# Two reorderings in a two-layer transformer kernel: value heads among the projections, and row scores behind a projection

## What is computed

```python
x = layernorm(x + attn0(x))   # 32 heads of width 16; the scores of a token are head against head
x = layernorm(x + ffn0(x))    # three dense layers with sign matrices, relu between
x = layernorm(x + attn1(x))   # 32 heads, rotary, causal, window of 128 tokens
x = layernorm(x + ffn1(x))    # 16 experts, top 2, and a shared expert

# attn0
q, k, v = (x @ w.T + b for each).reshape(1, 1024, 32, 16)
scores = einsum("bshd,bstd->bsht", q, k) / 4
context = einsum("bsht,bstd->bshd", softmax(scores), v)
```

## Time and profile before

| | us |
|---|---|
| runs before: median of 3 | 741.8 (741.8 to 742.43) |
| the profiled execution, its time | 742.59 |
| its span | 740.7 |
| PE busy | 618.5 (84%) |
| VectorE busy | 388.8 (52%) |
| ScalarE busy | 277.7 (37%) |
| GpSimd busy | 236.5 (32%) |
| mean granted clock of PE | 0.907 |

### The profile page before, as it was taken

How to read it: one execution, slowest core, us unless ns; L and a number is a source line. 1 busy time by engine, 2 the same in 40 slices (tenths; PEclk the granted TensorE clock), 3 DMA queues, 4 the chain that set the end, 5 groups by cost and what they waited for, 6 DMA issues and landing times.

```text
span 740.7 us, 13453 instructions
## 1 busy us (share of the span) xinstructions
PE 618.5 (84%) x5108; PEld 487.0 (66%) x5108; DVE 388.8 (52%) x1120; ACT 277.7 (37%) x439; POOL 236.5 (32%) x347
## 2 busy tenths in 40 slices
PE   2998996648889886989898987778689899999984
PEld 2997985536677664766676665556448688878761
DVE  4324345285776766758585766561546043322354
ACT  5156046356644143334342533344620022221313
POOL 6003422354200235445352634354005511111062
PEclk9999999688999986989898999576889999999997
DMA  8921213323016727263452719120005859997455
GB/s 292 401 94 34 50 31 100 79 56 94 1 60 153 141 74 145 79 95 114 61 144 31 171 40 213 22 67 23 1 1 177 334 198 395 418 417 291 184 169 185
DMA packets 49360, 104.37 MB, mean 141 GB/s; under 512 B 12113, under 2 KB 18385, under 8 KB 47761
## 3 DMA queue, kind: packets, MB, share of 16 engines
q1 hardware_dynamic: 30032, 61.68, 23.4%
q0 software_dynamic: 13744, 31.61, 18.8%
q10 hardware_dynamic: 5520, 10.23, 3.8%
HBM read 63.77 MB, written 35.13 MB: 134 GB/s over the span
## 4 chain that ended last, share of the span: by engine, by line
PE 56%; DVE 11%; DMA 11%; ACT 9%; issue 7%; POOL 6%; SPq 1%; POOLq 0%; ACTq 0%; DVEq 0%
PE bank L331 14%; PE bank L508 10%; PE bank L367 10%; ACT FP L1427 3%; DVE FP L902 3%; PE bank L594 3%; PE bank L579 3%; DMA slots_out<-FP 3%; PE bank L566 3%; PE bank L378 2%; POOL slots_in L1825 2%; POOL FP L1837 2%; DMA QS<-QS 2%; PE bank L389 2%; PE bank L709 2%
## 5 line engine op out<-in xcount | busy, mean ns | idle before, releaser
L1427 ACT ACTIVATE FP<-bank 128x512 f32<-128x512 f32 (+1 forms) x250 | 145.8, 624 | 324.2 <-PE bank L579 132.5
L1160 DVE CUSTOM_DVE_ANT_0 kraw<-bank,maskb 128x256 bf16<-128x256 f32 (+1 forms) x256 | 88.5, 401 | 60.6 <-PE bank L566 60.6
L508 PE MATMUL bank<-W,XR 128*128 128x512 f32 x348 | 106.0, 450 | 0.1
L331 PE MATMUL bank<-FP 128*128 128x128 f32 x558 | 87.5, 311 | 1.3 <-ACT FP L1427 1.3
L367 PE MATMUL bank<-W,XR 128*128 128x512 f32 x288 | 78.9, 420 | 6.1 <-DVE W L902 5.2
L508 PEld LDWEIGHTS bank<-W,XR 128*128 128x128 f32 x348 | 71.1, 216 | 16.3 <-DVE XR L902 0.5
L1789 POOL TENSOR_SCALAR_AFFINE_SELECT FP<-FP 128x512 f32<-128x512 f32 x64 | 41.4, 669 | 114.3 <-ACT FP L1427 114.3
L367 PEld LDWEIGHTS bank<-W,XR 128*128 128x128 f32 x288 | 63.7, 271 | 11.8 <-DVE W L902 5.6
L331 PEld LDWEIGHTS bank<-FP 128*128 128x128 f32 x558 | 65.2, 192 | 3.5 <-issue 1.8
L902 DVE TENSOR_TENSOR FP<-FP,bank 128x128 f32<-128x128 f32 (+1 forms) x39 | 14.4, 369 | 70.5 <-ACT FP L1427 45.7
L331 PE MATMUL bank<-RP,W 128*128 128x512 f32 x192 | 47.5, 404 | 4.4 <-DVE FP L902 2.2
(11 more groups left out here) (164 smaller groups left out, 1021.9 us busy)
## 6 DMA issues: line engine op xcount, KB each, us to landing
FP<-in_experts_dram SPq DMA_DIRECT2D x31, 768.0 KB, 7.1
slots_out<-QS SPq DMA_DIRECT2D x48, 256.0 KB, 2.7
FP<-slots_in POOLq DMA_DIRECT2D x31, 256.0 KB, 6.5
slots_out<-FP ACTq DMA_DIRECT2D x31, 256.0 KB, 7.7
slots_in<-RP SPq DMA_DIRECT2D x7, 1024.0 KB, 13.3
RP<-slots_out POOLq DMA_DIRECT2D x16, 384.0 KB, 5.7
QS<-slots_out POOLq DMA_DIRECT2D x10, 384.0 KB, 8.4
FP<-in_shared_dram SPq DMA_DIRECT2D x4, 768.0 KB, 7.5
```

The costliest lines, as they stand in the source:

```text
L331: mm = nc.tensor.matmul(bank, lhs, rhs, start=(n == 0), stop=(n == len(terms) - 1))
L508: mm = nc.tensor.matmul(b[:, :], *terms[n], start=(n == 0), stop=(n == len(terms) - 1))
L1160: ins = nc.vector.tensor_tensor_reduce(masked[:, 2 * (f % 2) + m, 0:n], b[:, m, :], maskb[:, m0:m0 + n], 1.0, -BIG, ALU.add, ALU.max, hmax ...
L1427: return nc.scalar.activation(o, i, func, **kw)
```

## The change

*First attention, TensorE.* Heads of keys of group 0 go three to a projection; the heads of values of group 0 go to the S banks, and the first two scores stand among the x transposes. Group 1's projections lie two to a step up to step 2 and one to a step in steps 3 to 6 (`tiles_of`); the heads of queries and keys stand two behind each third of a projection; the heads of values all stand in step 7, in V and A banks. VectorE drains the value heads of group 0 and two of the four of group 1 (`values_out`). *Key diagonals.* Five buffers: steps 0 to 9 use two as before, steps 10 to 15 three others (the third is zeroed by GpSimd after the last biased row), so SyncE waits for `scores(k - 3)` there. *ScalarE.* `ak` and `aq` are loaded in eight pieces of 256 KB behind step 9, 10, 11 and 12, not in step 4; `conn_weights(0)` moves ahead of the first statistics, `conn_weights(1)` goes one quarter to a step; the rounded pieces move to steps 13 and 14, beside `hidden(0, 1)`, and behind `hidden_out(1, 0, 0)`. GpSimd forms its eight remainders after step 15. *Second attention.* In iterations 0 to 5 `row_scores(r, 0)` stands behind the first projection; in iteration 6 (`late`) every row-score group comes one step later, with what follows from its maxima.

```diff
-        kdiag = [[t[:, a + 2048 * n:a + 2048 * n + 2048] for n in range(2)] for t, a in ((WF, 6 * DC * D), (FP, 0))]
+        kdiag = [t[:, a:a + 2048] for t, a in ((WF, 6 * DC * D), (WF, 7 * DC * D), (FP, 0), (FP, 2048), (RPF, 3264))]
...
+        def key_slot(k):
+            return (k % 2, k // 2 + 1) if k < NCH + 2 else (2 + (k - NCH - 2) % 3, (k - NCH - 2) // 3 + 1)
+        tiles_of = [tiles_between[a:b] for a, b in ((2, 4), (4, 6), (6, 8), (8, 9), (9, 10), (10, 11), (11, 12))]
# TensorE, first attention
             for j in range(G):
                 project(0, 2, j)
-                to_heads(V, 0, 1, 2 * j, 2 * j + 1)
+                to_heads(V, 0, 1, *range(3 * j, min(3 * j + 3, H // 4)))
...
-                to_heads(A, 0, 2, j, j + 1)
-            for k in range(2):
-                scores(k)
-                project(*tiles_between[k])
+                to_heads(S, 0, 2, j, j + 1)
+                scores(j // 2)
+            project(*tiles_between[0])
+            project(*tiles_between[1])
             for k in range(2 * NCH):
                 if k + 2 < 2 * NCH:
                     scores(k + 2)
-                between(k, 0)
-                if k in (6, 7):
-                    to_heads(V, 1, 2, 2 * k - 12, 2 * k - 11)
+                if k < 3:
+                    project(*tiles_of[k][0])
+                elif k < 5:
+                    for part in range(2):
+                        project(*tiles_of[k][0], 3 * part, 3)
+                        to_heads(V, 1, k - 3, 2 * part, 2 * part + 1)
+                elif k < 7:
+                    project(*tiles_of[k][0])
+                elif k == 7:
+                    for a in range(0, HD // 4, 2):
+                        to_heads(V, 1, 2, a)
+                        to_heads(A, 1, 2, a + 1)
...
                 values(k)
-                between(k, 1)
+                if k < 3:
+                    project(*tiles_of[k][1])
+                elif k < 5:
+                    for part in range(2, 4):
+                        project(*tiles_of[k][0], 3 * part, 3)
+                        to_heads(V, 1, k - 3, 2 * part, 2 * part + 1)
# TensorE, second attention (VectorE's row_maxima in the same way)
+                t, r, d, late = i + 2, i + 1, i - 1, int(i == T - 2)
                 for s in range(8):
-                    if r < T:
-                        row_scores(r, s)
+                    if r < T and (s > 0 or i < 0) and s >= late:
+                        row_scores(r, s - late)
...
                     if s < 2 and 2 <= t < T:
                         project2(t, 1 - s)
+                    if s == 0 and 0 <= i < T - 2:
+                        row_scores(r, 0)
...
+                if i == T - 2:
+                    row_scores(r, 7)
# SyncE
-                if k >= 2:
+                if 2 <= k < NCH + 2:
                     C.filled(sp, ("scores", k - 2))
+                elif k >= NCH + 5:
+                    C.filled(sp, ("scores", k - 3))
...
+                if k == NCH + 4:
+                    sp.wait_ge(diag_zero, 4)
...
-                if k == NCH + 5:
+                if k == NCH + 4:
                     load_kernel(1, k1)
# VectorE
+            def values_out(ring, g, a):
+                b = ring.take(v, ("heads", g, 2, a))
+                nc.vector.tensor_copy(vT[:, :, 4 * a:4 * a + 4].rearrange("p s h -> p h s"),
+                                      b[:, :].rearrange("p (h s) -> p h s", h=4)).then_inc(ring.free, 1)
# ScalarE
+            def load_piece(m):
+                n, c = (0, 2)[m // 4], m % 4
+                nc.scalar.dma_start(raw_c[n][:, c * D:(c + 1) * D], (ak, aq)[m // 4][c * P:(c + 1) * P, :]).then_inc(wc_in[n], 16)
...
             exponentials(NCH + 1)
-            high_piece(0)
-            high_piece(1)
+            C.filled(s, ("scores", NCH + 1))
+            conn_weights(0)
+            A.drained(s, ("heads", 1, 2, HD // 4 - 1))
+            load_piece(0)
+            load_piece(1)
             roots(slice(0, G), 0)
             exponentials(NCH + 2)
+            load_piece(2)
+            load_piece(3)
             s.wait_ge(offset_ready, 1)
             for t in range(G):
                 normalise(t)
-            conn_weights(0)
             for k in range(11, 2 * NCH):
                 exponentials(k)
+                if k <= 12:
+                    load_piece(2 * k - 18)
+                    load_piece(2 * k - 17)
...
-                if k <= 13:
-                    high_piece(2 * k - 20)
-                    high_piece(2 * k - 19)
-                if k == 14:
-                    conn_weights(1)
+                if k <= 14:
+                    conn_weights(1, k - 11)
+                if k in (13, 14):
+                    high_piece(2 * k - 26)
+                    high_piece(2 * k - 25)
...
-            hidden_out(0, 1, *range(DC))
-            high_piece(8)
-            high_piece(9)
+            for o in range(DC):
+                hidden_out(0, 1, o)
+                high_piece(4 + o)
...
-            high_piece(10)
-            high_piece(11)
+            for m in range(8, 12):
+                high_piece(m)
# GpSimd
+                if k == 7:
+                    A.drained(p, ("rows", 1, 2, G - 1))
+                    nc.gpsimd.memset(RPF[:, 3264:5312], 0.0).then_inc(diag_zero, 1)
+            for m in range(8):
+                low_piece(m)
```

More of the change, by code:

```diff
@@ L267, in build @@
         diag_zero = sem("diag_zero")
-        kdiag_in = [sem(f"kdiag_in{n}") for n in range(2)]
+        kdiag_in = [sem(f"kdiag_in{n}") for n in range(5)]
         kq_split = sem("kq_split")
@@ L383, in scores @@
                 g, c = chunk(k)
[L384 removed]
+                slot, n = key_slot(k)
+                pe.wait_ge(kdiag_in[slot], 16 * G * n)
                 b = C.fill(pe, ("scores", k))
[L386 removed]
+                keys = kdiag[slot].rearrange("p (j g a h) -> p j g a h", j=G, g=4, a=4)
                 for a in range(4):
@@ L656, in _ @@
                         A.drained(pe, ("ffn", T - 1))
-                    if s == 5 and r < T:
+                    if s == 5 + late and r < T:
                         turn_maxima(r, 0)
@@ L1055, in _ @@
                 low_xt(("x", G + j), every_fourth(j))
-            A.drained(v, ("heads", 0, 2, HD // 4 - 1))
-            shift(0)
+                if j == 1:
+                    for a in range(HD // 4):
+                        values_out(S, 0, a)
+                    shift(0)
             rows_biased(*tiles_between[0])
@@ L1224, in _ @@
             for i in range(-1, T):
-                t, r, d = i + 2, i + 1, i - 1
+                t, r, d, late = i + 2, i + 1, i - 1, int(i == T - 2)
                 for s in range(8):
-                    if r < T:
-                        row_maxima(r, s)
+                    if r < T and (s > 0 or i < 0) and s >= late:
+                        row_maxima(r, s - late)
                     if s < 2 and d >= 0:
                         context_divided(U, d, s)
+                    if s == 0 and 0 <= i < T - 2:
+                        row_maxima(r, 0)
                     if s == 1 and 2 <= t < T:
@@ L1239, in _ @@
                         rope_sum(t, 0)
-                    if s == 3 and r < T:
+                    if s == 3 + late and r < T:
                         maxima_split(r, 0)
@@ L1255, in _ @@
                         low_dense(("x2", t + 1), xa[t + 1][1], xa[t + 1][0])
-                    if s == 7 and r < T:
+                    if s == 7 and r < T and late == 0:
                         maxima_split(r, 1)
@@ L1484, in _ @@
             heads_out(V, 0, 1, *range(H // 4))
-            A.drained(s, ("rows", 0, 2, G - 1))
-            for j in range(0, G, 2):
+            for j in range(G):
                 high_x(G + j)
-                high_x(G + j + 1)
-                heads_out(A, 0, 2, j, j + 1)
             exponentials(0)
@@ L1728, in _ @@
             nc.gpsimd.memset(RPF[:, 0:3 * 1088], 0.0).then_inc(diag_zero, 1)
-            A.drained(p, ("heads", 0, 2, HD // 4 - 1))
+            S.drained(p, ("heads", 0, 2, HD // 4 - 1))
             p.wait_ge(pool, 3)
@@ L1744, in _ @@
                 if k == NCH:
-                    V.drained(p, ("heads", 1, 2, HD // 4 - 1))
+                    V.drained(p, ("heads", 1, 2, HD // 4 - 2))
+                    A.drained(p, ("heads", 1, 2, HD // 4 - 1))
                 for g in range(4):
@@ L1802, in _ @@
             for i in range(-1, T):
-                t, r = i + 2, i + 1
+                t, r, late = i + 2, i + 1, int(i == T - 2)
                 for step in range(8):
@@ L1817, in _ @@
                         stack_rows(t, 0)
-                    if step == 6 and r < T:
+                    if step == 6 + late and r < T:
                         stack_maxima(r, 0)
```

55 lines of the change are left out of this document (21 added, 34 removed).

## The result

The changed kernel is slower: 752.69 us, median of four runs (749.95 to 755.98), against 741.88 (741.8 to 742.43) for the kernel before. The ratio is 1.0146, 95% interval 1.0099 to 1.0193. The forecast was 744.8 in a range of 737 to 751: right in sign, too small in size, and the time is outside the range.

What follows compares the result with a forecast made beforehand. TensorE was 56% of the chain, losing time to first-attention diagonal waits. First half −11.1, second attention +11.8, clock +1.9, late form +0.4: +3.0 us on 742.59 gives 745.6, 744.8 as median; range 737 to 751.

Steps and rivals of the forecast that it cites:

- First attention: Whole first half: −6.7 up to values of step 8, −5.0 to step 15, +0.6 after; −11.1 us, range −6 to −14.
- The wait left: TensorE's 6.74 us wait for the key diagonal of step 8 was to shrink to 1.5 us.
- the third head's wait: Three key heads per projection, two V banks: the third head waits some 0.9 us, twice, costing 1.9 us.
- the wait for the value diagonal of step 8: First attention, TensorE: this wait, 4.29 us before, was to stay at some 4 us.
- The third buffer: Third key-diagonal buffer: removes the 3.42 us wait at step 14 and its issue behind the kernel load.
- Order of the transfers: Second attention boundaries: maxima stay behind the stack, so key scores start as now or slightly earlier; −0.85 us over six iterations.
- The counted cost of the pair: First and second row scores as neighbours wait for VectorE's maxima: 2.1 us an iteration, 12.6 us over six.
- The clock: Second attention: a slow-clock stretch behind about three of six new waits, adding +1.9 us.
- The rival that had the slow clock behind all six: Second attention: slow clock behind all six new waits, +5 in place of +1.9; 749 us, chance 0.06.
- the forecast's bound of 3.3: Upper bound, in us an iteration, on the row-score pair's cost, with a half-clock stretch behind each.
- the first: Rival: second half costs only 1.1 us an iteration, slack or later waits swallowing half; 737.5 us, chance 0.28.
- The late form: Iteration 6, row scores one step back: splits of shared weights start later, +0.4 us, bounds −1 and +2.

Runs made afterwards that it cites:

- the first half alone: Changed first attention, with the second attention as in the kernel before: 732.12 us, ratio 0.9857 to the kernel before.
- the run with the loads back: Changed first attention, second as before, with four weight pieces (1 MB) issued in step 4 again: 734.6 us, ratio 0.9879 to the kernel before.
- The run with SyncE's queue: Changed first attention, second as before except maxima transfers on SyncE's queue and first row scores behind 6 of 12 matmuls: 726.76 us, ratio 0.979.
- filler: Changed kernel plus seven matmuls between first and second row scores of iterations 0 to 5: 746.96 us, ratio 1.0073 to the kernel before.
- the second half alone: Changed second attention, with the first attention as in the kernel before: 766.06 us, ratio 1.0324 to the kernel before.

## Why the prediction was right or wrong

**First attention: right, in size and by its steps.** Forecast −11.1 us, measured −11.3 at tile 0 and −9.4 in the medians of the first half alone. Step 5 at 119.1, measured 119.27; step 7 at 130.1, its scores at 129.00; values of step 8 at 138.9, measured 138.60; of step 15 at 172.4, measured 172.43. The landing of 2 us was right (2.01), and the run with the loads back shows its cause. The wait left was 0.62 and not 1.5; the third head's wait 0.69 and not 0.9, twice; VectorE's head copies 1.04 to 1.09 us, not 0.9. Some of the agreement is luck: step 7 came 1.1 us sooner than worked out, and the wait for the value diagonal of step 8, put at some 4 us, took 5.16. The third buffer, priced at the 3.42 us that it removed, is worth some 4.6, for the clock behind its wait.

**Order of the transfers: right.** Key scores never start while the stack is awaited, and moving the row scores won no wait. The page "DMA: Bandwidth & Descriptors" of the Trainium skill, cited ahead, has the descriptors of one queue start in order; that they also land in order it does not promise. In the changed kernel the last transfer of the maxima, which the key scores need, lands 0.3 to 1.5 us behind the last of the stack, though the first of the two can land up to 0.3 us ahead of it. The run with SyncE's queue lies outside that rule; there too the last 8 KB land no sooner than the stack.

**The counted cost of the pair: right.** 1.8 us of wait forecast, 1.65 measured; 2.2 us from one group to the next, measured 2.15. With the clock kept up by filler, B is 13.4 us longer than before, forecast 12.6. That the six periods as a whole lose 11.5 us, forecast 11.8, is partly luck: A and C came out 1.9 shorter in that execution.

**The clock: this step failed.** The forecast added +1.9 us, "a slow stretch behind about three of six, most of a doubled projection being hidden by VectorE". The runs put 5.7 to 7.3 us there (B is 44.1 us in the second half alone and 45.7 in the changed kernel, against the filler's 38.4; the medians of the changed kernel and the filler differ by 5.7 too). So the term was three to four times too small, and both halves of the sentence were wrong. The slow stretches: behind five of the six new waits, not three, the second projection runs below full clock (3.84 to 4.61 us, full clock 2.98); the other period, of mean granted clock 0.93, is the cheapest (+1.8 us). The rival that had the slow clock behind all six priced it at 5 us and was nearer, with a chance of 0.06. Of the loss of 24.1 us, 20.7 are in B: 13.4 by the pair and 7.3 by the clock. The other 3.4 lie in A and C, where the forecast had −0.85; they stay open. Per iteration that is 4.0 us, beyond the forecast's bound of 3.3.

The second half of the sentence: VectorE does not hide the slow projection, since it isn't the engine that sets the pace at that place. Its timeline after the change:

```profile
329.65 0.42 DVE L1188 CUSTOM_DVE_ANT_0 kraw<-bank,maskb 128x256 bf16<-128x256 f32 x1 [4.54 <-PE bank L573]
...
331.77 0.42 DVE L1188 CUSTOM_DVE_ANT_0 kraw<-bank,maskb 128x256 bf16<-128x256 f32 x1 [0.66 <-PE bank L573]
...
337.25 0.28 DVE L1202 CAST QS<-bank 32x128 fp32r<-32x128 f32 x1 [0.90 <-PE bank L539]
```

VectorE waits for PE three times; the first wait was there before (3.99 us), the other two are new. The chain in order of time runs through both projections:

```profile
324.28 4.90 PE bank L515 x12
...
333.15 3.95 PE bank L515 x12
```

In the kernel before, PE at full clock was just ahead of VectorE there, as the earlier trace rows show with one idle piece of 0.43 us. Below full clock it falls behind. The argument "VectorE is the bound, so PE's speed is hidden" held only for the speed at which it was read.

A part that the forecast had no term for: at two boundaries of six (328.32 and 395.28) the group that was moved had broken up the boundary's wait, and after the change the wait is one piece (3.71 us with PE at 0.01). At 328.32 the first projection then takes 5.25 us and not 4.58, but at 395.28 it is 4.59 and not 4.93. Over the six the first projections take 29.0 us against 27.5. So this part is small, and that the unbroken wait is its cause is not shown.

**Two rivals' times** do not follow from their own terms: the first gives 736.8 us and not 737.5, the slow clock behind all six 747.9 and not 749.

**The late form:** +0.4 forecast, nothing measured in total; in its own period some 2 us, which come back behind tile 7.

## What to carry to other kernels

A wait of 1.65 us on TensorE cost 2.2 us with its group of matmuls, and some 1 us more by the low clock behind it. When an edit adds a wait behind a low-clock stretch, recompute PE's timeline at half clock before calling another engine the bound. If a small group must wait for a drain, put it into the middle of a long run of matmuls: here the wait was gone. And look at what else is in flight when a small transfer is late: 1.5 MB of loads that nobody needed yet cost this kernel some 7 us at one boundary.

## What the runs showed of the hardware that was not expected

The last 8 KB transfer of the maxima takes 1.91 us with no stack ahead. At the changed kernel's boundaries it takes 5.3 to 6.6 us, issued some 3 to 5 us behind a stack on the same queue, and 10.84 with the shared weights in flight too. From SyncE's queue, issued as the stack is, it takes 8.1 to 9.7 us. Seven matmuls that compute nothing useful, six times over (1.89 us each time), made the kernel 5.7 us faster in the medians (752.69 to 746.96).
